# A two-layer metaformer on one NeuronCore: the second and fourth norm in units of four images, with TensorE carrying the relayout

## The reference, cut to what matters

```
x = x + L0_conv(ln_c(x))          # norm 0: over the 64 channels of every pixel, eps 1e-6
t = tokens(x)                     # (16, 3600, 64)
t = t + L0_ffn(ln_t(t))           # norm 1: over the 64 channels of every token, eps 1e-5
x = x + L1_conv(ln_c(x))          # norm 2
t = t + L1_ffn(ln_t(t))           # norm 3
```

## Time and profile before

| | us |
|---|---|
| median of three runs | 4789.94 (4781.53 to 4798.68) |
| the profiled execution | 4773.51 |
| its span (first to last instruction) | 4771.5 |
| norm 0, its windows 28 to 146 and 146 to 173 | 145 |
| rows and columns of layer 0, 173 to 1024 | 851 |
| norm 1 with routing, 1024 to 1550 | 526 |
| experts, 1550 to 1609 | 59 |
| norm 2, 1609 to 1763 | 154 |
| rows and columns of layer 1, 1763 to 2612 | 849 |
| norm 3 with batch statistics, 2612 to 2865 | 253 |
| batch norm's constants and recurrence, 2865 to 4771 | 1906 |

### The profile page before, as it was taken

The page is one execution under the profiler, slowest core; times in us unless marked ns, Lnnn a source line. Parts: engine busy times, 40 slices in busy tenths (PEclk is TensorE's granted clock), DMA queues, the critical chain, the costliest instruction groups (busy, mean ns, idle before and its releaser), DMA issues.

```text
span 4771.5 us, 107854 instructions
## 1 busy us (share of the span) xinstructions
PE 4504.9 (94%) x41841; PEld 2802.6 (59%) x41841; DVE 1406.3 (29%) x2619; ACT 1702.4 (36%) x5935; POOL 105.9 (2%) x195
## 2 busy tenths in 40 slices
PE   7999999987777989999999899999999999999999
PEld 1699999963333549999999333333333333333333
DVE  3555533333433355553333561000000000000000
ACT  4102344464544220124444853333333333333333
POOL 1000000000000000000000000000000000000000
PEclk7799999997878789999999989999999999999999
DMA  4000000021213440000000530000000000000000
GB/s 119 16 0 0 0 0 0 0 54 47 54 47 79 139 121 0 0 0 0 0 0 9 143 92 13 16 16 16 16 16 9 15 16 16 16 16 16 16 16 12
DMA packets 151331, 139.01 MB, mean 29 GB/s; under 512 B 84158, under 2 KB 150750, under 8 KB 151262
## 3 DMA queue, kind: packets, MB, share of 16 engines
q1 hardware_dynamic: 151262, 138.22, 11.7%
HBM read 79.18 MB, written 58.98 MB: 29 GB/s over the span
## 4 chain that ended last, share of the span: by engine, by line
PE 89%; DVE 3%; ACT 3%; issue 3%; SPq 1%; DMA 0%; POOL 0%; ACTq 0%; DVEq 0%; POOLq 0%; PEldq 0%
PE ps L769 21%; PE ps L700 19%; PE ps L678 16%; PE ps L849 15%; PE ps L764 3%; PE ps L622 2%; PE ps L719 2%; PE ps L580 2%; ACT sums L947 2%; PE ps L590 1%; PE ps L568 1%; PE ps L636 1%; PE ps L756 1%; PE ps L742 1%; PE ps L732 1%
## 5 line engine op out<-in xcount | busy, mean ns | idle before, releaser
L769 PE MATMUL ps<-idle 128*32 128x512 bf16 (+1 forms) x5760 | 1598.8, 338 | 0.0
L849 PEld LDWEIGHTS ps<-xl,vt 65*32 65x32 f32 x14400 | 521.0, 108 | 1165.6 <-ACT xl L1061 1113.5
L1061 ACT ACTIVATE xl<-ps 64x16 f32<-64x16 f32 x3600 | 641.2, 178 | 1250.8 <-PE ps L849 1250.8
L700 PE MATMUL ps<-xl,taps 128*128 128x128 f32 (+2 forms) x7880 | 912.6, 279 | 4.7 <-DVE xl L1280 4.7
L700 PEld LDWEIGHTS ps<-xl,taps 128*128 128x128 f32 x7880 | 912.1, 191 | 5.6 <-issue 5.3
L849 PE MATMUL ps<-xl,vt 65*32 65x16 f32 x14400 | 871.2, 193 | 7.9
L678 PE MATMUL ps<-split 128*128 128x400 f32 x4140 | 782.0, 352 | 10.5 <-DVE split L1275 10.5
L678 PEld LDWEIGHTS ps<-split 128*128 128x128 f32 x4140 | 779.9, 190 | 14.3 <-issue 12.9
L1349 DVE TENSOR_TENSOR xl<-xl 64x480 f32<-64x480 f32 x120 | 116.5, 970 | 1776.8 <-PEq L846 889.2
L919 ACT ACTIVATE img<-xl 128x144 f32 x788 | 366.1, 465 | 547.5 <-DVE xl L1257 547.5
L1257 DVE SCALAR_TENSOR_TENSOR xl<-ps,img 128x144 f32<-128x144 f32 x788 | 323.8, 411 | 587.8 <-PE ps L700 587.8
(11 more groups left out here) (144 smaller groups left out, 2250.0 us busy)
## 6 DMA issues: line engine op xcount, KB each, us to landing
ring<-in_x_dram SPq DMA_DIRECT2D x72, 200.0 KB, 3.4
ring<-in_x_dram SPq DMA_DIRECT2D x144, 100.0 KB, 2.4
t_dram<-sums SPq DMA_DIRECT2D x144, 100.0 KB, 2.2
ring<-t_dram SPq DMA_DIRECT2D x72, 200.0 KB, 3.8
x_dram<-sums SPq DMA_DIRECT2D x72, 200.0 KB, 3.4
ring<-x_dram SPq DMA_DIRECT2D x144, 100.0 KB, 2.4
x_dram<-sums SPq DMA_DIRECT2D x144, 100.0 KB, 2.2
xl<-x_dram SPq DMA_DIRECT2D x30, 480.0 KB, 6.3
```

Of the source, the lines that this page charges most:

```text
L700: last = pe.matmul(acc[:, :, lo:hi], taps[:, (k * NO + d + 2) * 128:(k * NO + d + 3) * 128], column[h][:, :, lo + d:hi + d], start=(n == 0 ...
L769: pe.matmul(PS[2][0:32, 0:n], idle[:, 0:32], idle[:, 0:n], start=True, stop=True)
L849: last = pe.matmul(PS[s][c * 32:(c + 1) * 32, t * B:(t + 1) * B], vt[:, c * 32:(c + 1) * 32], prev, start=False, stop=True, skip_group_che ...
L1061: act.activation(yb[0:64, s % 2, :, t], PS[s % 2][0:64, t * B:(t + 1) * B], ACT.Sigmoid).then_inc(step_y, 1)
```

## The change

Norms 1 and 3 are written anew after the pattern of norms 0 and 2, and some smaller things change beside it.

- **Units.** Norm 1 and norm 3 now have 36 units of 2 x 400 columns (four images). A group is nine of them. The loops are written out.
- **The relayout moves to TensorE.** `move` copies a unit out of the column layout into two PSUM banks by four matmuls with a 64x64 identity block (K = 64, M = 64, 400 columns). VectorE adds the input from `ring` straight out of PSUM (`total`, two instructions of 128x400) and puts the rows into natural order by the access pattern `by_rows`. ScalarE's four copies for each chunk are gone.
- **Statistics.** One Sqrt and one reciprocal of 128x400 for each group of four images take the place of 64-row pieces and of the split into high and low parts; the spread is two fp32 matmuls of 32 rows. The sums of squares are 32-column matmuls for two units at a time.
- **Norm 1** takes nine units of means, then the reciprocal, then nine times spread and logits in turn. The logits are four matmuls of K = 64, M = 32 instead of two full ones.
- **Norm 3** takes the spread 12 and the product 13 units behind the mean; the product has one bank (`PRODUCT`), so product and `bn_stats` take turns.
- **The last group** of norms 0, 2 and 3 has 7 or 6 banks for the spread instead of 2.
- **Clock matmuls.** 16 `keep_clock` before norm 0, one for every pair of units in norm 0, and 14 ahead of the wait for the reciprocal: in the last group of norms 0, 2 and 3 and in each group of norm 1.
- **Set-up.** 8 wider `affine_select` in place of 40; the fp32r copy is gone; TensorE waits for `spread_ready` only before the first spread. The squares of norms 1 and 3 lie in `taps`, which GpSimd clears again before layer 1. `tt` has its own buffer.

The diff, cut to its core (the functions that it removes are in the listing above; `kept_tokens` and `normed_tokens` are views of where a unit's tokens lie):

```diff
-        sq = sb("sq", [128, 2 * CH])
-        rparts = ctx.enter_context(nc.sbuf_tensor("rparts", [128, 2 * CH], fp32r))
-        spread = ctx.enter_context(nc.sbuf_tensor("spread", [128, 5 * 128], fp32r))
-        tt = sums[0:TC, 0:RING * 384]
-        tt_pool = sq[:, 0:128]
+        token_squares = [taps[:, j * CH:(j + 1) * CH] for j in range(TOKEN_SQUARES)]
+        tt = sb("tt", [TC, RING * 384])
+        average = sb("average", [128, 128])
+        tt_pool = average[:, :]
...
+        LAST_SPREAD = (6, 7, 0, 1, 2, 4, 5)
+        LAST = (NG - 1) * NCH
+
+        def spread_bank(n, h):
+            return SPREAD32[h] if n < LAST else LAST_SPREAD[(2 * (n - LAST) + h) % len(LAST_SPREAD)]
...
+        TOKEN_XC, PRODUCT, MOVE = (0, 1), 2, (4, 5)
+        ROUTE_SPREAD = (6, 7, 0, 1)
+        TOKENS_LAST = (6, 7, 0, 1, 4, 5)
+        KEPT = NCH + 4
+        def token_spread_bank(i, n, v):
+            j = 2 * n + v
+            if i == 1:
+                return ROUTE_SPREAD[j % len(ROUTE_SPREAD)]
+            return SPREAD32[v] if n < LAST else TOKENS_LAST[(j - 2 * LAST) % len(TOKENS_LAST)]
...
+        def by_rows(t, hp):
+            return t.rearrange("p (q e j w) -> p q e w j", e=2, j=WP, w=2)[:, :, hp, :, :]
...
-                for p in range(0, 10, 2):
-                    for h in range(2):
-                        part = ones_at[:, p * 64 + h * 64:p * 64 + (h + 1) * 64]
-                        alone(pool.affine_select(out=part, in_=part, compare_op=ALU.not_equal, fill=1.0, base=-(32 * q + p + h),
-                                                 pattern=[[0, 64]], channel_multiplier=1))
-            pool.tensor_copy(spread[:, :], ones_at)
+                for h in range(2):
+                    part = ones_at.rearrange("p (k x) -> p k x", x=128)[:, :, h * 64:(h + 1) * 64]
+                    alone(pool.affine_select(out=part, in_=part, compare_op=ALU.not_equal, fill=1.0, base=-(32 * q + h),
+                                             pattern=[[-2, 5], [0, 64]], channel_multiplier=1))
...
+            pool.wait_ge(ln[1].var, 2 * UNITS)
+            pool.memset(taps[:, :], 0.0).then_inc(taps_blank, 1)
...
+        def variances(pe, i, n, squares):
+            st, g, k = ln[i], n // NCH, n % NCH
+            if k % 2 == 0 and k < NCH - 1:
+                return
+            pe.wait_ge(st.squared, 2 * n + 2)
+            if k == 1 and g:
+                pe.wait_ge(st.std, g)
+            for m in ((n - 1, n) if k % 2 else (n,)):
+                km = m % NCH
+                c0 = 126 - 2 * (km // 2)
+                for h in range(2):
+                    q = 2 * (km % 2) + h
+                    pe.matmul(PS[VAR][32 * q:32 * q + 32, 0:CH], pick[:, c0:c0 + 32], squares[(2 * m + h) % len(squares)],
+                              start=(km < 2), stop=(km >= NCH - 2)).then_inc(st.var, 1)
+            if i == 0:
+                keep_clock(pe, 512, SPARE)
+        def spread_one(pe, i, n, h, bank):
+            st, g, k = ln[i], n // NCH, n % NCH
+            p, q = 2 * (k // 2), 2 * (k % 2) + h
+            pe.matmul(PS[bank][:, 0:CH], spread32[32 * q:32 * q + 32, p * 64:p * 64 + 128],
+                      rstd[32 * q:32 * q + 32, (g % 2) * CH:(g % 2 + 1) * CH], start=True, stop=True).then_inc(st.spread, 1)
+        def pe_token_norm(pe, i):
+            def move(n):
+                for hp in range(2):
+                    if n:
+                        pe.wait_ge(st.summed, 2 * n + hp - 1)
+                    for h in range(2):
+                        last = pe.matmul(PS[MOVE[hp]][h * 64:(h + 1) * 64, 0:CH], half(ident, hp)[:, hp * 64:(hp + 1) * 64],
+                                         half(rows_of(i, n, h), hp), start=True, stop=True)
+                    last.then_inc(st.moved, 1)
+            def take_mean(n):
+                pe.wait_ge(st.summed, 2 * n + 2)
+                for v in range(2):
+                    j = 2 * n + v
+                    if j >= 2:
+                        pe.wait_ge(st.kept, j - 1)
+                    pe.matmul(PS[TOKEN_XC[v]][:, 0:CH], centre[:, :], unit_of(sums, n % RING)[:, v * CH:(v + 1) * CH],
+                              start=True, stop=True).then_inc(st.centred, 1)
+            def spread_out(n):
+                g, k = n // NCH, n % NCH
+                banks = ROUTE_SPREAD if i == 1 else TOKENS_LAST if n >= LAST else SPREAD32
+                since = 2 * NCH * g if i == 1 else 2 * LAST if n >= LAST else 0
+                if k == 0:
+                    if i == 1 or n == LAST:
+                        pe.wait_ge(st.kept, 2 * (n + NCH))
+                        for _ in range(14):
+                            keep_clock(pe, 512, MOVE[1])
+                    pe.wait_ge(st.inverse, g + 1)
+                for v in range(2):
+                    j = 2 * n + v
+                    if j - since >= len(banks):
+                        pe.wait_ge(st.normed, j - len(banks) + 1)
+                    elif j >= 2 and i == 3:
+                        pe.wait_ge(st.normed, min(j - 1, 2 * LAST))
+                    spread_one(pe, i, n, v, token_spread_bank(i, n, v))
+            def logits(n):
+                g, k = n // NCH, n % NCH
+                if k >= 2:
+                    pe.wait_ge(st.taken, n - 1)
+                pe.wait_ge(st.normed, 2 * n + 2)
+                for v in range(2):
+                    for h in range(2):
+                        q = 2 * v + h
+                        last = pe.matmul(PS[MOVE[k % 2]][q * 32:(q + 1) * 32, 0:CH], half(gate, h)[:, v * 192 + h * 32:v * 192 + h * 32 + 32],
+                                         half(xl, h)[:, v * S + k * CH:v * S + (k + 1) * CH], start=True, stop=True)
+                last.then_inc(st.mixed, 1)
+            def product(n, v):
+                j = 2 * n + v
+                if j:
+                    pe.wait_ge(st.taken, j)
+                pe.wait_ge(st.normed, j + 1)
+                for o, t in normed_tokens(i, n, v):
+                    last = pe.matmul(PS[PRODUCT][:, o:o + t.shape[-1]], wbd[:, :], t, start=True, stop=True)
+                last.then_inc(st.mixed, 1)
+            for h in range(2):
+                pe.wait_ge(put_back[i // 2][h], 1 + STEPS[2] + STEPS[3])
+            if i == 1:
+                for g in range(NG):
+                    first = g * NCH
+                    if g:
+                        pe.wait_ge(st.taken, first)
+                    move(first)
+                    for n in range(first, first + NCH):
+                        if n + 1 < first + NCH:
+                            move(n + 1)
+                        take_mean(n)
+                        if n > first:
+                            variances(pe, i, n - 1, token_squares)
+                    variances(pe, i, first + NCH - 1, token_squares)
+                    for n in range(first, first + NCH + 1):
+                        if n < first + NCH:
+                            spread_out(n)
+                        if n > first:
+                            logits(n - 1)
+                    pooling(pe, g)
+                return
+            move(0)
+            for n in range(UNITS + LAG + 1):
+                m = n - LAG - 1
+                if LAG <= n < UNITS + LAG:
+                    spread_out(n - LAG)
+                if m >= 0:
+                    product(m, 0)
+                if n + 1 < UNITS:
+                    move(n + 1)
+                if n < UNITS:
+                    take_mean(n)
+                if m >= 0:
+                    product(m, 1)
+                if 0 < n <= UNITS:
+                    variances(pe, i, n - 1, token_squares)
...
+                    if n == LAST:
+                        pe.wait_ge(st.kept, 2 * UNITS)
+                        for _ in range(14):
+                            keep_clock(pe, 512, SPARE)
+                    elif i == 0 and n == 0:
...
+            for _ in range(16):
+                keep_clock(pe, 512, SPARE)
...
+            def keep(n):
+                for v in range(2):
+                    j = 2 * n + v
+                    xc = PS[TOKEN_XC[v]][:, 0:CH]
+                    act.wait_ge(st.centred, j + 1)
+                    if j >= TOKEN_SQUARES:
+                        act.wait_ge(st.var, j - TOKEN_SQUARES + 1)
+                    act.activation(token_squares[j % TOKEN_SQUARES], xc, ACT.Square).then_inc(st.squared, 1)
+                    if i == 3 and v and n >= KEPT:
+                        act.wait_ge(st.normed, 2 * (n - KEPT) + 2)
+                    for o, t in kept_tokens(i, n, v):
+                        last = act.activation(t, xc[:, o:o + t.shape[-1]], ACT.Copy)
+                    last.then_inc(st.kept, 1)
...
+            def total(n):
+                unit_free(dve, i, n)
+                for hp in range(2):
+                    dve.wait_ge(st.moved, 2 * n + hp + 1)
+                    moved = PS[MOVE[hp]][:, 0:CH].rearrange("p (q w j) -> p q w j", w=2, j=WP)
 ```

(24 more changed lines are left out.)

397 lines of the change are left out of this document (90 added, 307 removed).

## The result

The changed kernel takes 4546.07 us (median of four, 4541.29 to 4550.77) against 4785.73 for the kernel before in the same comparison: ratio 0.9523, 95% interval 0.9495 to 0.9551. Faster, as forecast, but by 240 us where I had 178.5, and outside my range. The profiled execution of after took 4550.77 us (span 4549.0) against 4773.51, so 222.7 us can be followed stage by stage.

| us | before | after | change | forecast |
|---|---|---|---|---|
| start and norm 0 | 172.8 | 144.1 | -28.7 | -19.5 |
| sweeps, layer 0 | 850.4 | 850.2 | -0.2 | 0 |
| norm 1 with routing | 527.0 | 377.7 | -149.3 | -125 |
| experts | 58.7 | 58.5 | -0.2 | 0 |
| norm 2 | 154.0 | 147.7 | -6.3 | -10 |

A forecast was written before the change was run, and what follows sets the result against it. Norm 1's adds wait for ScalarE's copies and TensorE for the adds; TensorE is full in steady norm 3. Terms -125 - 24 - 20 - 9.5 = -178.5, from 4789.9 to 4611 us; range 4570 to 4650, with rivals 4565 to 4700.

The forecast's parts named there:

- I add 6 a group: Norm 1: 6 us a group, 24 in all, added for half clock, cold start and DMA load.
- 9 for semaphore distances: Norm 1: of -134 us only -125 counted, leaving 9 for semaphore distances missing from the sum of starts.
- ScalarE's copies as the cause: Norm 1's norms and logits: VectorE's adds stand idle 219 us for ScalarE's copies, and TensorE waits for the adds.
- Norm 3: Norm 3: 39 + 125 + 11 + 48 = 223 us, with small waits 229, against 253: -24.
- the 6 for small waits: Norm 3: 6 us added for small waits to the sum of 223, making 229.
- Start and norm 0: Start -9.5 us, first square at 21.2; norm 0's last group -10; idle matmuls inside norm 0 taken as 0.
- Last groups of norms 0 and 2: Spread and VectorE's scalings overlap with seven banks, 2 x 0.57 us a unit instead of 2.36: -10 each, -20.
- The scale: Whole kernel: median of the runs 16.4 us above the profiled execution of 4773.5, so the forecast starts from 4789.9.
- loads: Rival: norm 1's first halves and norm 3's first twelve units go at 3.5 us, +24, 4635 us; chance 0.10.
- the move without overlap: Rival: the move's four matmuls run one after another, +2.2 us a unit over 72 units, +160, 4771; chance 0.03.
- Half clock in the thin phases: Rival: half clock in norm 1's spread and logits, +48 us, and norm 3's last nine units, +15: 4674; chance 0.17.
- mode changes: Norm 3: five tiling-mode changes a unit, before six; at 0.05 us each the sum 2 better, by rows alone unchanged.

The follow-up runs named there:

- the doubled move: The changed kernel with every move done twice (eight 64x64 matmuls of 400 columns a unit into the same banks): 4606.37 us, +60.3.

## Why the prediction was wrong

The miss is 65 us: 44 in the sum and 21 in the scale.

- **Norm 1: the step that failed is "I add 6 a group", with the "9 for semaphore distances".** The sum before them was nearly right: 48.5 and 3 x 51 make 201.5, and the four groups took 46.8, 49.0, 49.0 and 50.1 from their first move to the end of their logits, 195. The 33 us of allowance for half clock, cold start, DMA and semaphores were not there. Half clock was kept out of the logits by the fourteen idle matmuls, as the runs without and with seven of them show, though three of 48 groups in other profiles did lose it; the loads did not bind, as the doubled move shows. In the other direction I had costed the routing's change at nothing, and it grew by 15 us, from 4 x 41.4 to 181: mostly one pooling, here the third, that stayed at half clock (54.6 us where the first two took 43).
- **ScalarE's copies as the cause**: half right. They were what the adds, and TensorE behind them, waited for, but taking them back costs 51 of the 149 us, not most of it.
- **Norm 3:** 229 forecast, 219.8 measured. The start and the first twelve units took 38.2 where I had 39: they went at 2.8 and not at norm 2's 3.1, but began later. The 24 units with all parts took 131.1 where I had 125 and 11 for two reciprocal stalls; 24 x 5.19 leave 6.5 for the stalls, as work without gaps behind a wait of 2.42 us was at full clock again after about 4 us. The tail took 50.5 where I had 48, and the 6 for small waits were not there. The other 3 of the 12 us are the border: norm 3 before is 255.8 by the table above, where I had 253.
- **Start and norm 0:** -28.7 against -19.5. The first square came at 23.23, not 21.2, so the start gave 7.5 and not 9.5. The last group gave 12 and not 10. The remaining 9 lie in norm 0's body, which I had at zero. The idle matmuls are worth about 4 and 6 us there by the medians, each within what these comparisons can tell; that they are the whole of the 9 is not shown, and norm 0 varies by as much among profiles of kernels that do not differ in it (137.7 to 146.5).
- **Last groups of norms 0 and 2:** -10 each forecast; 26.3 us each became 14.4 and 14.7, -12 each, and taking the banks back cost 20.8 for both. Norm 2 as a whole gained only 6.3, as the units ahead of its last group took 5 us more in this profile; norm 2 took 140.5 to 148.5 in the other profiles with the same norm 2, so that is within what it varies.
- **The scale:** I put the median 16.4 above the profiled execution because it was so in three runs of before. Over 36 further runs its median is 4776.3, only 3 above. The gap was luck, and the changed kernel's profiled run lay 4.7 above its own median instead.
- **Rivals:** loads (by the doubled move) and the move without overlap (it takes 0.83) are out. Half clock in the thin phases did not happen here but is real. Of mode changes, the doubled move is the first row that shows a price: four 64x64 matmuls cost 0.83 behind a full one and 0.69 behind their like, 0.14 more. By the Trainium skill, *TensorEngine Tiling (Array Packing)*, Key Properties, a mode change drains the engine; this agrees, though the start of a stream would look the same, so it is not shown that the drain is the cause. As both kernels change mode about as often, the sum does not move.

## What to carry to other kernels

Where TensorE is the bound, add the distances of starts and stop: an allowance on top needs a row of its own, as a term left out does. Before a thin stretch, fill TensorE's wait with idle matmuls as far as it goes, and read the clock behind it in more than one profile, since the same wait can keep the clock in one and lose it in another. Look for waits of that kind that the change does not touch: here the routing's four waits gave more than the seven banks in the last groups of norms 0 and 2 (27 against 21 us). Give a copy to the engine that has room in that stretch; the same relayout belongs on TensorE in norm 1 and on ScalarE in the steady part of norm 3.

## What the hardware showed that I had not expected

- Half clock in a stretch that TensorE still fills mostly can last: 57 us behind one wait of 3.27 us (busy 48 of 56 us there), 37 us in one pooling behind 12.43 us of idle, while other poolings behind the same idle had full clock again after 9 us.
- What idle loses the clock is not a matter of its length alone: behind seven idle matmuls 1.61 us kept full clock (norm 3) and 1.90 us lost it (norm 1); behind fifty, 1.54 or 1.55 us kept it in all sixteen poolings of the four versions that have them; behind fourteen, 1.11 us and then 1.12 us lost it in three of 48 groups.
- Eighteen matmuls more ahead of TensorE's loop, with their weight loads, made 60 passes of the recurrence 16.2 us longer (1917.7 against 1901.5), one wait of about 0.4 us a pass; the old number of matmuls gave it back, while 200 more or 20 fewer than in the changed kernel had cost nothing. Why a loop's place should cost is open.
